# A depthwise-plus-pointwise convolution and a sign convolution: sharing the centre-row products of the low weights

## The reference

```
x = x + einsum(G, einsum(pw, einsum(A, depthwise3x3(gn(x)))))    # A, G: softmax of 64x64 weights
x = x + conv3x3(sign(gn(x)), sign(w) * mean|w|)                 # 64 -> 64 channels
gn: 32 groups of 2 channels, mean and variance over the 2 channels and all pixels
```

## Time and profile before

| | |
|---|---|
| median of three runs | 1845.02 us |
| span of the profiled execution | 1841.7 us |
| TensorE busy | 1763.1 us (96%) |
| TensorE weight loads busy | 1571.6 us (85%) |
| VectorE busy | 1596.8 us (87%) |
| ScalarE busy | 1333.7 us (72%) |
| GpSimd busy | 580.3 us (32%) |
| DMA, mean rate | 147 GB/s |

### The profile page before, as it was taken

One profiled execution on the slowest core, in us unless ns is written; L12 is line 12 of the kernel. 1 busy time (PEld: TensorE's weight loads), 2 busy tenths in 40 slices (PEclk: granted clock), 3 DMA queues, 4 the chain that ended last, 5 costly groups with the idle time before them and its releaser, 6 DMA issues.

```text
span 1841.7 us, 76040 instructions
## 1 busy us (share of the span) xinstructions
PE 1763.1 (96%) x33132; PEld 1571.6 (85%) x33132; DVE 1596.8 (87%) x2581; ACT 1333.7 (72%) x1460; POOL 580.3 (32%) x353
## 2 busy tenths in 40 slices
PE   0499999999999999999999999999999999999997
PEld 0499998998799998999989888898989999899886
DVE  6888899888989889888898888988899888977776
ACT  2377777777677777777777777777767777777774
POOL 1233333333233332333333333333323332333331
PEclk9999999999999999999999999999999999999999
DMA  9735655566556565556656655556655666333324
GB/s 303 181 105 161 159 148 152 161 154 154 145 145 172 153 153 146 155 161 159 153 146 162 157 151 150 143 167 159 150 150 150 163 157 157 96 82 80 77 72 104
DMA packets 278623, 271.37 MB, mean 147 GB/s; under 512 B 16112, under 2 KB 278320, under 8 KB 278464
## 3 DMA queue, kind: packets, MB, share of 16 engines
q1 hardware_dynamic: 269568, 260.11, 54.4%
q10 hardware_dynamic: 8448, 8.39, 1.5%
q0 software_dynamic: 448, 0.73, 0.2%
HBM read 134.95 MB, written 134.22 MB: 146 GB/s over the span
## 4 chain that ended last, share of the span: by engine, by line
PE 95%; SPq 2%; DVE 1%; DMA 1%; issue 0%; ACT 0%; DVEq 0%; ACTq 0%
PE psA L520 82%; PE psB L520 13%; SPq L263 2%; DMA ring<-in_x 1%; DVE ring L964 0%; PE psL L485 0%; DVE psL L960 0%; PE psL L478 0%; DVE bnt L749 0%; DVE ring L969 0%; DVE aggr L865 0%; DVE xh L989 0%; ACT rnd L424 0%; DVE xc L922 0%; DVEq L111 0%
## 5 line engine op out<-in xcount | busy, mean ns | idle before, releaser
L520 PE MATMUL psA<-xh,W 64*64 64x512 f16 x17912 | 1550.9, 373 | 5.8 <-DVE xh L989 5.8
L520 PEld LDWEIGHTS psA<-xh,W 64*64 64x64 f16 x17912 | 1120.4, 106 | 101.1 <-issue 41.3
L520 PE MATMUL psA<-xl,W 64*64 64x512 f16 x9216 | 987.9, 376 | 0.0
L315 POOL TENSOR_TENSOR xl<-xc,xn 128x1024 f16<-128x1024 f32 (+1 forms) x320 | 570.7, 1793 | 1185.6 <-ACT xn L392 1173.6
L520 PEld LDWEIGHTS psA<-xl,W 64*64 64x64 f16 x9216 | 599.3, 107 | 25.5 <-issue 0.6
L520 PE MATMUL psB<-pk,W 64*64 64x512 f16 (+2 forms) x4944 | 608.2, 362 | 2.0 <-DVE pk L941 1.9
L396 ACT ACTIVATE xh<-xc 64x1024 f16<-64x1024 f32 (+2 forms) x622 | 574.4, 941 | 9.2
L392 ACT ACTIVATE xn<-xc 128x1024 f16<-128x1024 f32 (+2 forms) x262 | 270.7, 1036 | 269.3 <-PE psA L520 183.1
L930 DVE SCALAR_TENSOR_TENSOR ring<-psA,columns,ring 128x1024 f32<-128x1024 f32 x256 | 328.3, 1282 | 124.5 <-PE psA L520 124.0
L520 PEld LDWEIGHTS psB<-pk,W 64*64 64x64 f16 x4944 | 305.6, 106 | 61.0 <-issue 35.5
L749 DVE BATCH_NORM_STATS2 bnt<-ring 128x6 f32<-128x512 f32 x512 | 325.8, 681 | 35.0 <-DMA ring<-in_x 34.8
(11 more groups left out here) (101 smaller groups left out, 106.0 us busy)
## 6 DMA issues: line engine op xcount, KB each, us to landing
out_y<-ring SPq DMA_DIRECT2D x512, 256.0 KB, 3.3
ring<-in_x SPq DMA_DIRECT2D x448, 256.0 KB, 4.0
ring<-in_x SPq DMA_DIRECT2D x16, 512.0 KB, 16.8
ring<-in_x ACTq DMA_DIRECT2D x16, 512.0 KB, 15.9
pk<-in_w1T POOLq DMA_DIRECT2D x2, 144.0 KB, 6.2
ring<-in_w1n POOLq DMA_DIRECT2D x2, 144.0 KB, 6.9
grp<-in_same_group POOLq DMA_DIRECT2D x1, 64.0 KB, 7.3
ring<-in_dw POOLq DMA_DIRECT2D x2, 2.2 KB, 6.7
```

Source lines behind the costliest of these rows:

```text
L315: ins = nc.gpsimd.tensor_tensor(xl[:, slot:slot + rows, 1:W + 1], xc[:, j:j + rows], xn[:, k:k + rows, 1:W + 1], ALU.subtract)
L520: mm = pe.matmul(bank[out0:out0 + C, c0:c1], weights[src0:src0 + C, :], src[src0:src0 + C, slot:slot + rows, width[0]:width[0] + width[1]] ...
```

## The change

- TensorE: the product of the low weights with the centre row is the same for both rows of a pair up to what it is added to. The low weights are rewritten as differences to the centre block (`W0l[:, :, 0]`, `W0l[:, :, 3]`), and the centre block is multiplied once with the sum of neighbouring rows, `sh` (`shared_rows`, slots 19 to 21, crossing). Its result goes from the PSUM bank `psP` through ScalarE (`keep_shared`, fp16 `pf`) and is added into both rows by a product with a scaled identity (`add_shared`, slot 3 of the next step). A step has 31 slots. `first_row` adds half-width products in the first chunk of an image.
- VectorE: `sums_high` builds `sh` from `xn` and `xh` at the head of a step; `pack` leaves; `left` is kept as fp16 in `rnd` where it was in PSUM (`psL`), whose bank is now `psP`. `a_mm`, which `add_layer0` waits for, comes from slot 3 of the next step.
- ScalarE: no longer writes `xh` (but for the first chunk of all); writes 1536 times the right half into `pk`, and copies `psP` into `pf`.
- GpSimd: adds the left half to `pk`. `sg` has one buffer where it had two.
- SyncE: `swap_high(t+1)` copies `xn` into `xh` with the halves swapped, SBUF to SBUF, two or four DMAs per chunk, ahead of the load and the store of the step.
- The ring has 40 chunks, and the statistics run 34 chunks ahead. `stats_parts` is in step 29, `stats_of_group` and `scale_of_group` both in step 30; `border_of_group` comes behind the normalise.
- The loops of TensorE and GpSimd are written out.

```
-RING = 41
+RING = 40
-BEFORE = 35
+BEFORE = 34
-WEXP = 2.0 ** 14
+WEXP = 2.0 ** 13
+PSCALE = 2.0 ** 12
...
+    def shared(ch):
+        return G - 1 if ch.at(NC - 1) else G
+    def swaps(ch):
+        return (([(0, 0, 1)] if ch.at(0) else []) + [(G * ch.q + 1, 1, shared(ch))] + again(ch))
...
-    AGGR_STEP, GROUP_STEP, SCALE_STEP = NC - 4, NC - 3, NC - 2
+    AGGR_STEP, SCALE_STEP = NC - 3, NC - 2
...
+            def swap_high(n):
+                ch = Chunk(n % NC)
+                sp.wait_ge(xn_rdy, n + 1)
+                if n >= 2:
+                    sp.wait_ge(products_done, n - 1)
+                for (i0, i1), (o0, o1) in ((LO, HI), (HI, LO)):
+                    for slot, j, rows in swaps(ch):
+                        k = buf(ch, j)
+                        sp.dma_start(xh[o0:o1, slot:slot + rows, :],
+                                     xn[i0:i1, k:k + rows, :]).then_inc(xh_in[n % 2], 16)
...
             for t in range(ALL):
+                if t + 1 < ALL:
+                    swap_high(t + 1)
                 if RING <= t + RING - LAG - 2 < ALL:
                     load_chunk(t + RING - LAG - 2)
...
+            nc.gpsimd.tensor_tensor(W0l[:, :, 0:3], W0t, W0h[:], ALU.subtract).then_inc(lo_rdy, 1)
+            pool.wait_ge(lo_rdy, 1)
+            nc.gpsimd.tensor_tensor(W0l[:, :, 0], W0l[:, :, 0], W0l[:, :, 1], ALU.subtract)
+            nc.gpsimd.tensor_tensor(W0l[:, :, 3], W0l[:, :, 2], W0l[:, :, 1], ALU.subtract).then_inc(w_rdy, 1)
...
+            def pack(n):
+                pool.wait_ge(right_rdy, n + 1)
+                for slot, j, rows in packed(Chunk(n % NC)):
+                    here = pk[:, slot:slot + rows]
+                    ins = nc.gpsimd.tensor_tensor(here, here, sg[:, j:j + rows, 0:HPW], ALU.add)
+                ins.then_inc(pk_rdy, 1)
...
+                    act.wait_ge(products_done, n - 1)
                     act.wait_ge(xl_rdy, n - 1)
+                    act.wait_ge(sh_rdy, n - 1)
...
-                for (i0, i1), (o0, o1) in ((LO, HI), (HI, LO)):
-                    for slot, j, rows in together(ch):
-                        ins = nc.scalar.activation(xh[o0:o1, slot:slot + rows, 1:W + 1], xc[i0:i1, j:j + rows],
-                                                   ACT.Copy)
-                ins.then_inc(xh_rdy, 1)
...
-                    act.wait_ge(pk_rdy, n if ch.at(1) else n - 1)
+                    act.wait_ge(pk_rdy, n)
...
+                for slot, j, rows in packed(ch):
+                    ins = nc.scalar.activation(pk[:, slot:slot + rows], sg[:, j:j + rows, HW:PW], ACT.Copy,
+                                               scale=PACK)
+                ins.then_inc(right_rdy, 1)
+            def keep_shared(n):
+                act.wait_ge(sums_done, n + 1)
+                if n > 0:
+                    act.wait_ge(a_mm, n)
+                at = 2 * n % 4 * W
+                nc.scalar.activation(pf[:, at:at + 2 * W], psP, ACT.Copy, scale=1.0 / PSCALE).then_inc(pf_rdy, 1)
...
             for t in range(ALL):
                 if t + 1 < ALL:
-                    high_of(t + 1)
+                    high_part(t + 1)
+                if t % NC == SCALE_STEP and t // NC + 1 < NB:
+                    square_root(t // NC + 1)
                 if t + 1 >= LAG:
-                    signs_of(t + 1 - LAG)
+                    signs(t + 1 - LAG)
+                keep_shared(t)
                 if t >= LAG:
-                    round_of(t - LAG)
+                    round_b(t - LAG)
...
+            def crossing(t, k):
+                ch = Chunk(t % NC)
+                if k < 3:
+                    own_high(ch, 1, k, True, k == 0)
+                elif k == 3:
+                    if t > 0:
+                        pe.wait_ge(products_done, t)
+                        pe.wait_ge(pf_rdy, t)
+                        add_shared(t - 1, True)
+                elif k < 7:
+                    own_rest_natural(ch, k - 4)
+                elif k < 10:
+                    if k == 7:
+                        pe.wait_ge(xl_rdy, t + 1)
+                    own_low(ch, 1, k - 7)
+                elif k < 13:
+                    mm = beside_low(ch, 1, k - 10)
+                    if k == 12:
+                        mm.then_inc(cross_left, 1)
+                elif k < 19:
+                    if t >= LAG:
+                        crossing_signs(t - LAG, k - 13)
+                elif k < 22:
+                    if k == 19:
+                        pe.wait_ge(sh_rdy, t + 1)
+                        if t > 0:
+                            pe.wait_ge(pf_rdy, t)
+                    mm = shared_rows(ch, k - 19)
+                    if k == 21:
+                        mm.then_inc(sums_done, 1)
+                else:
+                    if k == 22:
+                        pe.wait_ge(straight_left, t + 1)
...
+            def straight(t, k):
+                ch = Chunk(t % NC)
+                if k < 3:
+                    own_high(ch, 0, k, False, k == 0)
+                elif k == 3:
+                    if t > 0:
+                        add_shared(t - 1, False).then_inc(a_mm, 1)
...
+                else:
+                    mm = centre_low(ch, 1, k - 28)
+                    if k == 30:
+                        mm.then_inc(products_done, 1)
...
+                    pe.wait_ge(xh_in[t % 2], xh_count(t))
+                if t >= 2:
+                    pe.wait_ge(a_post, t - 1)
+                for k in range(31):
+                    crossing(t, k)
+                    straight(t, k)
+                    if a == 0 and k == 10:
+                        mean_average(img)
+                    if a == SCALE_STEP and k == 4 and img + 1 < NB:
+                        gather_stats(img + 1)
...
+            def sums_high(n):
+                ch = Chunk(n % NC)
+                rows, lo = shared(ch), G * ch.q + 1
+                if n > 0:
+                    dve.wait_ge(xn_rdy, n + 1)
+                    dve.wait_ge(xh_in[n % 2], xh_count(n))
+                    dve.wait_ge(sums_done, n)
+                k = buf(ch, 1)
+                nc.vector.tensor_tensor(sh[:, 0:rows], xn[:, k:k + rows], xh[:, lo:lo + rows],
+                                        ALU.add).then_inc(sh_rdy, 1)
...
-                return (here, rnd[:].bitcast(I16)[:, :, 0:2 * HW:2],
-                        psL[:, ch.par, 0:G * HW].rearrange("p (s w) -> p s w", s=G))
+                return here, rnd[:].bitcast(I16)[:, :, 0:2 * HW:2], rnd[:].bitcast(F16)[:, :, 1:2 * HW:2]
...
             for t in range(ALL):
                 img, a = divmod(t, NC)
+                sums_high(t)
                 if t > 0:
                     add_layer0(*of(t - 1))
+                if a == SCALE_STEP and img + 1 < NB:
+                    stats_of_group(img + 1)
...
-                if t + 1 >= LAG:
-                    pack(*of(t + 1 - LAG))
...
                 if t + 2 < ALL:
+                    dve.wait_ge(xl_rdy, t + 2)
                     normalise(*of(t + 2))
+                if a == SCALE_STEP and img + 1 < NB:
+                    border_of_group(img + 1)
```

463 lines of the change are left out of this document (207 added, 256 removed).

## The result

The changed kernel takes 1893.9 us (median of four runs, 1884.7 to 1910.6) against 1844.9: a ratio of 1.0276, 95% interval 1.0228 to 1.0324. It is slower, as forecast, but by 49 us where I had 8, and outside my range of 1828 to 1876. The span of its profiled execution is 1893.6 us.

What follows compares the result with a forecast made beforehand. TensorE, busy 96% of the span, was taken as the bound. Slots -27.6, `first_row` +2.6, changes of image +29.4, start +1 and end +3.2 gave +8.6 us: span 1850.3, time 1853, range 1828 to 1876.

Steps and rivals of the forecast that it cites:

- TensorE's own work: TensorE's step falls to 31 slots, 6.71 us, 0.108 less: -27.6 us over 256 steps; new waits inside it cost nothing.
- VectorE's terms: VectorE in mid-image: pack leaves, the fp16 sum (0.73) and blocking by GpSimd (0.28 and 0.13) come; it still hides.
- the rival of 1.17: VectorE becomes the bound: the sum at the slow pace, 1.17 us, makes its loop 6.9; 1900 us, chance 0.12.
- The loop of 6.44: VectorE's mid-image loop after the change takes 6.44 us, under TensorE's 6.71, with 0.27 to spare.
- The swapped halves by DMA: SyncE's swap in mid-image: 0.65 us per issue, 2.5 to land, last landing at 4.65 or 5.95, before 6.71; hides.
- the load slips by 1.3 us: SyncE's load, queued behind the swap, slips 1.3 us and keeps more than 1 us before its statistics.
- The swap doesn't hide in mid-image: Rival: every fourth step late by 0.1 to 1 us, +6 to +60; no chance of its own, widens the range.
- The change of image: Chain VectorE, ScalarE, swap: TensorE waits 4.2 us for the first chunk at seven changes, +29 us (+18 to +38).
- the gather's 0.9: At the change of image TensorE's gather matmul waits 0.9 us for the statistics, inside the same 4.2.
- Ends: Start of the kernel +1 us (0 to 4); end +3.2, as the last signs wait for GpSimd's pack.
- the whole sum: Whole kernel: -27.6 + 2.6 + 29.4 + 1 + 3.2 = +8.6 us on the span 1841.7, to 1850.3.
- the 3.3 us that I added from span to time: Whole kernel: the median of runs before, 1845.0, lay 3.3 us above the profiled span; added to reach 1853.

Runs made afterwards that it cites:

- e4: Changed kernel with each load half waiting only for the same half of the store that emptied its place: 1857.1 us, ratio to before 1.0064.
- e1: Changed kernel with the swaps issued by ScalarE behind `xn`, SyncE keeping loads and stores: 1939.2 us, ratio to before 1.0497.
- e6: Changed kernel with `xh` written by ScalarE again and no swap issued: 1947.8 us, ratio to before 1.0559.
- e8 to e14: Changed kernel with edits at the change of image (first chunk's `xh` by ScalarE, reordering, statistics moved), all but one with e4's waits: 1845.0 to 1893.6 us.
- e5: Changed kernel storing a quarter of the bytes, the rest of the output left out: 1853.3 us, ratio to before 1.0042.
- e7: Changed kernel with the loads that reuse a ring place issued by GpSimd: 1965.2 us, ratio to before 1.0656.

## Why the prediction was wrong, point by point

*TensorE's own work* was right. I had 6.71 us a step; undisturbed steps take 6.70 to 6.73 after (113 of the 192 in the middle of an image), and 6.71 in e4. The wait on `pf_rdy` at slot 3 breaks nothing in mid-image.

*VectorE's terms* were right. The sum L998 takes 0.71 us in the mean, and 0.61 from its start to the next (I took 0.73 for that; the rival of 1.17 falls). L1025, the old L964, is stretched beside GpSimd: 1.04 in the mean against 0.75, I had 1.03. L1030, the old L969, has 0.86 for 0.81, where I had added 0.13. The loop of 6.44 fits as well: in e4 VectorE idles 0.21 and 0.38 us before the two L1006 shown, where I had 0.27 to spare. One reading was off and moved nothing: `xh` was ready 3.25 us before its use in mid-image, not 3.4 (903.59, and the next step starts at 906.84).

```profile
L1025 DVE SCALAR_TENSOR_TENSOR ring<-rnd,smalls,ring 128x512 f32<-128x512 f16 x256 | 265.3, 1036 | 9.1
...
L1030 DVE SCALAR_TENSOR_TENSOR ring<-rnd,smalls,ring 128x512 f32<-128x512 int16 x256 | 218.9, 855 | 0.2
...
L998 DVE TENSOR_TENSOR sh<-xn,xh 128x1032 f16<-128x1032 f16 (+1 forms) x256 | 181.9, 710 | 21.0 <-issue 13.0
```

*The swapped halves by DMA* is the step that failed: "In mid-image this hides too, with 0.7 us to spare in every fourth step", and behind it "the load slips by 1.3 us and still has more than 1 us before its statistics". In its place mid-image steps took 6.77 to 7.20 us, image by image, where I had 6.71, because TensorE waited for the swapped halves: some 42 us. I priced the swap as a line from `xn` to TensorE and the load as a line to its statistics, and I counted SyncE's issues (3.9 to 5.2 us of 6.71) as if issuing were all that it did. The load's slip by itself did little: VectorE's waits for loads went from 34.8 to 40.3 us in the whole run. What failed has two parts:
1. Not seen: SyncE's loop store, landing, load, store. Its row stood in the trace of before, in SyncE's waits, and I didn't put it into the sum:

```profile
SPq L239 <- DMA out_y<-ring: 650.0, 215, 4.9
```

In 215 of its steps SyncE waited there, 3.0 us at a time. With two issues of the store, that wait and two issues of the load the loop is 1.3 + 3.0 + 1.3 = 5.6 us, under 6.82 with 1.2 to spare, and harmless. With the longest wait, 4.9, it would be 7.5.
2. Mis-sized: landings taken as they were before. The swaps add bytes (a mean of 182 GB/s for 147), and they are issued right behind the store. With them the store's landing goes from 3.3 to 3.8 us in the median, and in the slow stretch to 4.9 to 5.2 for the second half (4.34 behind the end of its issue, and the 0.65 of that). Which of the two, the bytes or the place in the queue, lengthens it more was not tried apart, but e1 bears on it: with the same bytes and no swap in SyncE's queue the stores' median is still 3.6, and in e6, without swaps, it is 3.3 again. The swap lands after 3.0 (I took 2.5), and its issues take 0.76 in the mean where I took 0.65 (the 3.69 for four above is near the longest; the median of four is 2.95).

```profile
out_y<-ring SPq DMA_DIRECT2D x512, 256.0 KB, 3.8
ring<-in_x SPq DMA_DIRECT2D x448, 256.0 KB, 4.0
xh<-xn SPq DMA_DIRECT2D x494, 129.0 KB, 3.0
xh<-xn SPq DMA_DIRECT2D x126, 32.2 KB, 2.7
```

I had a rival for this ("The swap doesn't hide in mid-image": late by 0.1 to 1 us, "+6 to +60"), which holds the 42 us. I gave it no chance of its own and let it only widen the range, to 1876, so the measured time lies outside what I stated.

*The change of image* was about right in size and in its signs. I had one wait of 4.2 us in seven places, the gather's 0.9 within it. e4 shows 1.14 and 2.0 to 3.2, in sum 3.1 to 4.3. Images take 221.0 us in the mean in e4 (starts of `add_layer0`, 32 steps apart) where 219.1 of before, less the slots, plus `first_row` and 4.2 gave 220.2: 0.8 more an image, 5.5 us in seven. What I had wrong there is that it's one chain through the swap: the runs e8 to e14 show three, of nearly the same length.

*Ends.* The last L1005 of the kernel after starts 19.5 us before the end, L930 of before 17.1: +2.4, I had +3.2. The rounding that I placed 6.2 us behind it stands at 6.0 (1880.14, 1874.14). The first steps cost 1.4 to 1.6, I had 1.

```profile
1874.14 1.28 DVE L1005 SCALAR_TENSOR_TENSOR ring<-psA,smalls,ring 128x1024 f32<-128x1024 f32 x1 [2.92 <-PE psA L653]
...
1880.14 0.67 ACT L486 ACTIVATE rnd<-psB,smalls 128x512 f32<-128x512 f32 x1
```

With the loop open the whole sum can be tested: I forecast a span of 1850.3 and a time of 1853; e4 has 1856.6 and 1857. The span is the fairer comparison, 6.3 us off, nearly all of it at the changes of image: the 3.3 us that I added from span to time are 1.8 in each run of the changed kernel and of e4, which happens to bring the times closer. The other 37 us of the changed kernel are the loop.

## What to carry to other kernels

A queue that issues in order and waits for landings is an engine with a loop: write its period down (issue, landing, the issue that waits for it, and back), and compare it with the step before anything is put on the queue or more bytes on the DMA engines. A queue's waits of 650 us are harmless only while they are slack. The row that names the culprit is late by nature: TensorE waited for the swap, the loop was closed by the store.
When two transfers go out one behind the other, let each reader wait for its own half. That cost nothing here and was worth 37 us.
Where several chains of nearly one length end in one place, removing one is worth at most its distance to the next. Look for the next before pricing it.

## What the runs showed of the hardware

- The landing time of these small transfers is mostly not bytes: SBUF-to-SBUF swaps of 129 and of 32 KB land after 3.0 and 2.7 us, and with a quarter of the stored bytes (e5) after 2.4 and 2.0; a store of 64 KB takes 2.4 there. The Trainium skill, page DMA: Bandwidth & Descriptors, section Anatomy of one DMA, gives a constant part of about 2.0 us per transfer, for another issuing path. With its rate an estimate for the two swaps is 2.3 and 2.1 us: e5's trace agrees within 0.1, and the busier changed kernel lies 0.6 to 0.7 above it.
- Landings of stores of one size differ with what else is moved, but not by the mean rate alone: 3.3 us at 147 GB/s (before) and at 141 (e6), 3.8 at 182 (after), 3.6 at 186 (e4) and at 178 (e1), 4.4 at 176 with the loads issued by GpSimd (e7).
- An issue of a swap costs ScalarE as much as SyncE: in e1 1.27 us for two and 2.71 for four in the median (up to 2.46 and 4.09), in e4 on SyncE 1.28 and 2.57 (up to 2.54 and 3.72).
- VectorE beside GpSimd: the instruction that is 0.3 us longer in the mean took 1.96 us in e4 at the change of image, where VectorE came later than usual and GpSimd was subtracting until 955.02. The Trainium skill, page SBUF — State Buffer, section Summary: rules for kernel authors, has the later one blocked fully when VectorE's has two SBUF inputs and GpSimd's reads SBUF. The rows agree: from GpSimd's end to VectorE's, at 955.56, it is 0.5 us, less than the 0.75 of the shortest such instruction, so it was held nearly to that end. No run here took GpSimd's part away.

```profile
952.32 2.70 POOL L356 TENSOR_TENSOR xl<-xc,xn 128x256 f16<-128x256 f32 x2 [4.23 <-ACT xn L444]
...
953.60 1.96 DVE L1026 SCALAR_TENSOR_TENSOR ring<-rnd,smalls,ring 128x512 f32<-128x512 f16 x1
```
